# Attention and state-space block on one core: decays spread by DMA instead of by products with selecting rows

## The reference, cut to what matters

```python
dt = softplus(zxbcdt[..., -NHEADS:] + dt_bias)          # per token and head
A = -jnp.exp(A_log)
def step(state, inp):
    dt_t, x_t, B_t, C_t = inp
    dA = jnp.exp(dt_t * A)                               # the decay of this token, per head
    state = state * dA[:, :, None, None] + (dt_t[:, :, None] * x_t)[..., None] * B_t[:, None, None, :]
    y_t = jnp.einsum('bhpn,bn->bhp', state, C_t)
```

## Time and profile before

| | |
|---|---|
| median of 3 runs | 303.43 us (301.35 to 304.26) |
| the profiled execution | 301.26 us, span of its instructions 299.2 us |
| TensorE busy | 270.4 us, 90% |
| VectorE busy | 247.0 us, 83% |
| ScalarE busy | 207.6 us, 69% |
| GpSimd busy | 105.1 us, 35% |
| moved by DMA | 7.32 MB |

### The profile page before, as it was taken

How to read it: one execution, slowest core, us unless ns; L and a number is a source line. 1 busy time by engine, 2 the same in 40 slices (tenths; PEclk the granted TensorE clock), 3 DMA queues, 4 the chain that set the end, 5 groups by cost and what they waited for, 6 DMA issues and landing times.

```text
span 299.2 us, 6186 instructions
## 1 busy us (share of the span) xinstructions
PE 270.4 (90%) x2006; PEld 226.1 (76%) x2006; DVE 247.0 (83%) x537; ACT 207.6 (69%) x406; POOL 105.1 (35%) x113
## 2 busy tenths in 40 slices
PE   3999998999979999999999999997999897967781
PEld 3878996897868878887888788986798884555681
DVE  6695658787999979786899788858999999999943
ACT  1346779869868876968977787768674579777252
POOL 7000115600180614334333237116010519554552
PEclk9999999999999999999999999999999999999996
DMA  6910000000000000000000000000000100000103
GB/s 175 412 59 3 0 3 0 2 0 0 2 2 3 0 2 0 2 0 3 1 2 0 2 0 1 3 2 0 2 0 0 41 33 2 0 2 1 70 2 141
DMA packets 3787, 7.32 MB, mean 24 GB/s; under 512 B 652, under 2 KB 1581, under 8 KB 3757
## 3 DMA queue, kind: packets, MB, share of 16 engines
q1 hardware_dynamic: 3212, 6.72, 6.0%
q10 hardware_dynamic: 544, 0.21, 0.3%
HBM read 4.83 MB, written 2.10 MB: 23 GB/s over the span
## 4 chain that ended last, share of the span: by engine, by line
PE 66%; DVE 17%; issue 8%; ACT 5%; POOL 3%; DVEq 0%; ACTq 0%; POOLq 0%
PE mamba L1075 20%; PE scores L1075 17%; PE attn_out L1075 15%; PE turn L1148 7%; PE turn L1075 3%; DVE L L990 2%; DVE neg_max L900 2%; DVE th L1027 1%; DVE sp_sum L795 1%; POOL pre L524 1%; PE mamba L1166 1%; PE mamba L1207 1%; DVE L L1002 1%; DVE scanned L1010 1%; DVE res L911 1%
## 5 line engine op out<-in xcount | busy, mean ns | idle before, releaser
L1075 PE MATMUL attn_out<-values,pT 128*128 128x129 f32 x512 | 65.8, 276 | 2.5 <-DVE res L911 2.4
L1075 PEld LDWEIGHTS attn_out<-values,pT 128*128 128x128 f32 x512 | 62.2, 191 | 7.3 <-issue 4.9
L598 ACT ACTIVATE probs<-scores,neg_max 128x512 f32<-128x512 f32 x64 | 42.9, 686 | 24.6 <-DVE neg_max L900 22.2
L900 DVE TENSOR_REDUCE neg_max<-scores 128x1 f32<-128x1024 f32 x32 | 38.9, 1216 | 10.1 <-PE scores L1075 9.5
L990 DVE TENSOR_TENSOR_SCAN L<-mamba,ident 128x512 f32<-128x512 f32 x32 | 38.7, 1216 | 5.9 <-PE mamba L1075 5.7
L604 ACT ACTIVATE pT<-turn 128x512 f32<-128x512 f32 x64 | 37.6, 596 | 6.5 <-PE turn L1148 6.4
L1148 PE MATMUL turn<-ident,probs 128*128 128x128 f32 x256 | 37.9, 274 | 0.4 <-issue 0.2
L1148 PEld LDWEIGHTS turn<-ident,probs 128*128 128x128 f32 x256 | 30.2, 142 | 5.4 <-issue 3.2
L1075 PE MATMUL scores<-h_hi,q_hi 128*128 128x512 f32 x64 | 28.8, 451 | 2.7 <-ACT probs L598 1.2
L524 POOL TENSOR_TENSOR pre<-pre,th 128x512 f32<-128x512 f32 x16 | 20.7, 1292 | 27.6 <-ACT pre L630 22.2
L1075 PE MATMUL scores<-h_hi,q_lo 128*128 128x512 f32 x64 | 25.3, 395 | 0.0
(11 more groups left out here) (204 smaller groups left out, 613.9 us busy)
## 6 DMA issues: line engine op xcount, KB each, us to landing
res<-in_x_tok SPq DMA_DIRECT2D x4, 512.0 KB, 8.2
out<-res SPq DMA_DIRECT2D x8, 256.0 KB, 2.0
x_all<-in_x SPq DMA_DIRECT2D x3, 512.0 KB, 8.6
x_all<-in_x SPq DMA_DIRECT2D x2, 256.0 KB, 3.1
winT<-in_in_wT SPq DMA_DIRECT2D x1, 194.0 KB, 7.0
wqkv<-in_qkv_w ACTq DMA_DIRECT2D x1, 192.0 KB, 4.1
wpT<-in_proj_wT SPq DMA_DIRECT2D x1, 64.0 KB, 3.6
ob_row<-in_proj_b SPq DMA_DIRECT2D x1, 64.0 KB, 6.2
```

The source lines that it names most:

```text
L598: act.activation(probs[:, i % 2, half_of(h)], scores[:, half_of(h)], ACT.Exp, bias=neg_max[:, i:i + 1]).then_inc(exp_done.sem, 1)
L900: V.tensor_reduce(neg_max[:, n:n + 1], scores[:, :], AX.X, ALU.max, negate=True).then_inc(max_ready.sem, 1)
L1075: return T.matmul(o, w, v, start=start, stop=stop)
```

## The change

The decays are transposed on TensorE directly from dA, without the split in two parts. ScalarE copies the 32 rows (16 decays, 16 decays since the chunk's start, each of 128 tokens) to SBUF ("rows"), SyncE stores them to a scratch in DRAM ("wr", 16 KB), and per chunk one DMA reads four of the rows, 2 KB, and writes them to all 128 partitions of L, 256 KB ("bc"). The scan "l" reads L and writes L in place. For decay_in four DMAs per half batch ("dd", 64 KB each) write each head's rows to its 32 partitions. The zero at the start of each head now comes from the exponential: a bias of -1000 on the first partition, that is on the first token of a chunk. The steps dA_rows, dA_T, L, Dec and decay, the selecting rows and the mask are gone. ORDER is written anew throughout, with wr, bc, dd and the stores of the result ("store") as steps of SyncE, and other banks.

```diff
+                if kind == "wr":
+                    wait(sp, rows_ready, b, n + 1)
+                    sp.dma_start(rows_d[b, n], decay_rows[:, n, :]).then_inc(rows_out[n].sem, 16)
+                elif kind == "bc":
+                    wait(sp, rows_out[n // QUAD], b, 16)
+                    wait(sp, filled["Y"], b - 1, n // QUAD + 1)
+                    c = n % QUAD
+                    sp.dma_start(L[:, HEADS * n:HEADS * (n + 1), :].rearrange("p h i -> p (h i)"),
+                                 rows_d[b, n // QUAD, HEADS * c:HEADS * (c + 1), :].rearrange("(a h) i -> a (h i)", a=1)
+                                 .broadcast_to([P, HALF])).then_inc(spread[n].sem, 16)
+                elif kind == "dd":
+                    wait(sp, rows_out[n], b, 16)
+                    wait(sp, yo_ready, b - 1, n + 1)
+                    for h in range(HEADS):
+                        sp.dma_start(decay_in[h * HEADDIM:(h + 1) * HEADDIM, half_of(n)].rearrange("d (c i) -> d c i", c=QUAD),
+                                     rows_d[b, n, R:2 * R, :].rearrange("(a c h) i -> h a c i", a=1, h=HEADS)[h]
+                                     .broadcast_to([HEADDIM, QUAD, P])).then_inc(decay_in_ready[n].sem, 16)
...
-                    act.activation(dA[:, n, 0:R], la[:, n, :], ACT.Exp, scale=1.0 / A_SCALE).then_inc(dA_ready.sem, 1)
+                    act.activation(dA[:, n, 0:R], la[:, n, :], ACT.Exp, bias=first[:, :], scale=1.0 / A_SCALE
+                                   ).then_inc(dA_ready.sem, 1)
...
-                elif kind == "decay":
-                    wait(act, yo_ready, b - 1, n + 1)
-                    bank = take(act, b, "Dec", n)
-                    act.activation(decay_in[:, half], bank[:, :], ACT.Copy).then_inc(decay_ready.sem, 1)
+                elif kind == "rows":
+                    wait(act, rows_out[n], b - 1, 16)
+                    bank = take(act, b, "DAT", n)
+                    act.activation(decay_rows[:, n, :], bank[0:2 * R, 0:P], ACT.Copy).then_inc(rows_ready.sem, 1)
...
-                elif kind == "dA_rows":
...
-                elif kind == "dA_T":
...
                 elif kind == "l":
-                    wait(dve, filled["Y"], b - 1, n // QUAD + 1)
-                    bank = take(dve, b, "L", n)
-                    V.tensor_tensor_scan(L[:, HEADS * n:HEADS * (n + 1), :].rearrange("p a b -> p (a b)"), bank[:, :],
-                                         ident4[:, :, :].rearrange("p a b -> p (a b)"), 0.0, ALU.mult, ALU.add
+                    wait(dve, spread[n], b, 16)
+                    chunk = L[:, HEADS * n:HEADS * (n + 1), :].rearrange("p a b -> p (a b)")
+                    V.tensor_tensor_scan(chunk, chunk, ident4[:, :, :].rearrange("p a b -> p (a b)"), 0.0, ALU.mult, ALU.add
                                          ).then_inc(l_ready.sem, 1)
...
                 elif kind == "DAT":
-                    wait(pe, dA_rows_step, b, 2 * n + 2)
+                    wait(pe, dA_ready, b, n + 1)
+                    wait(pe, dec_ready, b, n + 1)
                     bank, done = fill(pe, b, "DAT", n)
-                    T.transpose(bank[:, 0:P], dA_rows[:, n, :], ident[:, :]).then_inc(done, 1)
+                    T.transpose(bank[:, 0:P], dA[:, n, :], ident[:, :]).then_inc(done, 1)
...
-                elif kind == "Dec":
...
-                elif kind == "L":
```

More of the change, by code:

```diff
@@ L184, in build @@
         neg_half = sb("neg_half", [P, TILES])
[L185 to L188, removed]
+        first = sb("first", [P, 1])
         x_all = sb("x_all", [P, BATCH * TOKENS])
@@ L439, in _, with step @@
                 sp.dma_start(res[:, b, :, :], x_tok[b]).then_inc(res_in[b].sem, 16)
-            for b in range(BATCH):
-                for n in range(2):
+            def step(kind, n, b):
+                if kind == "wr":
[15 more added lines that the diff above has]
+                                     .broadcast_to([HEADDIM, QUAD, P])).then_inc(decay_in_ready[n].sem, 16)
+                elif kind == "store":
                     four = slice(QUAD * n, QUAD * (n + 1))
@@ L447, in _ @@
                     sp.dma_start(out[b][:, four, :], res[:, b, four, :]).then_inc(out_sent[n].sem, 16)
+            for kind, n, b, _ in STEPS:
+                step(kind, n, b)
             for n in range(2):
@@ L760, in _ @@
             V.tensor_scalar(center[:, :], ident[:, :], 1.0 / P, None, ALU.subtract)
-            rows = ident[:, 0:4 * R].rearrange("r (s k c h) -> r k s c h", s=2, k=2, c=QUAD)
-            for k in range(2):
-                V.tensor_reduce(row_head[:, k, :], rows[:, k].rearrange("r s c h -> r h s c"), AX.XY, ALU.add)
-                last = V.tensor_reduce(row_chunk[:, k, :], rows[:, k].rearrange("r s c h -> r c s h"), AX.XY, ALU.add)
-            step_done(last)
-            V.tensor_copy(pick_chunk[:, :], row_chunk[:, 0, :])
-            V.tensor_copy(head_sel[:, :, :], row_head[:, 1, :].unsqueeze(2).broadcast_to([P, HEADS, HEADDIM]))
-            V.tensor_copy(head_mask[:, :, 0], row_chunk[:, 1, :])
-            step_done(V.tensor_tensor(head_mask[:, :, 1:P], row_head[:, 0, :].unsqueeze(2).broadcast_to([P, HEADS, P - 1]),
-                                      row_chunk[:, 1, :].unsqueeze(2).broadcast_to([P, HEADS, P - 1]), ALU.add))
-            dve.wait_ge(consts_done.sem, 9 + TERMS)
-            def rows_split(rows, value, signal, b, n):
-                k = value.shape[1]
-                V.tensor_copy(rows[:, 0:k].bitcast(F32R), value).then_inc(signal.sem, 1)
-                wait(dve, signal, b, 2 * n + 1)
-                V.tensor_tensor(rows[:, k:2 * k], value, rows[:, 0:k], ALU.subtract).then_inc(signal.sem, 1)
+            step_done(V.tensor_scalar(first[:, :], ident[:, 0:1], FIRST_BIAS, None, ALU.mult))
+            dve.wait_ge(consts_done.sem, 9 + TERMS)
             def softplus(b, n, k):
@@ L947, in step @@
                         wait(dve, sp_step, b, SP_STEPS * n + k)
+                    if k == SP_DT - 1:
+                        wait(dve, xdt_ready, b - 1, n + 1)
                     if k == SP_STEPS - 1:
```

187 lines of the change are left out of this document (86 added, 101 removed).

## The result

The changed kernel takes **307.05 us** in the median of 4 runs (305.94 to 307.35), the kernel before 302.39 beside it (301.32 to 304.26): a ratio of 1.0141, 95% interval [1.0074, 1.0207]. It is slower by 1.4%. I had predicted 296 us and given "slower" 0.37. (Ratios here leave disturbed runs out, so that they can differ a little from the quotient of two medians.)

A forecast was written before the change was run, and what follows sets the result against it. TensorE was taken as the bound from 10 to 220 us, VectorE after 245. 301.3 - 9.6 - 0.5 - 2.1 - 0.7 + 4.5 + 2.0 = 294.9, raised to 296 for half the return to the median; range 285 to 340.

The forecast's parts named there:

- TensorE, removed: L and Dec products gone: -9.6 us before 220 us (three quarters of 12.8), -0.5 between 220 and 245.
- The way through DRAM: Longer path from decays to scan by store and spread, nearly covered by other work: +2 us, bounds 0 and +8.
- the queue that I had set at nothing: SP's queue: its extra stores, spreads and small transfers delay nothing that is needed sooner: 0.
- The shared reading: Scans with two SBUF inputs stall beside GpSimd, mostly from 248 to 271 us: +4.5 us, bounds 0 and +7.
- VectorE's removed copies: After 245 us, where VectorE is the bound, two masked copies and four small steps go: -2.1 us.
- The start: Without the selecting rows and mask, the statistics of x begin earlier: -0.7 us, bounds 0 and -1.3.
- The hot row: Rival: spreads are slow because 128 partitions read the same DRAM row; +43, 339 us; chance 0.28.
- its worst form: Spreads cost by bytes, 12 us each, making the queue itself the bound: over 450 us; chance 0.07.
- rival (2): More scans beside GpSimd, whose waits lengthen the convolution's chain: +7 on the forecast, 303 us, no change; chance 0.15.
- wrong altogether would be a new bound that I haven't priced: Closing sentence on what would refute the forecast; its example was the SP queue held by a wait; no size.

The follow-up runs named there:

- e5: Kernel before, old order, with the 32 L and 8 Dec products run over 16 columns instead of 512: 306.52 us, ratio 1.0074.
- e3: Kernel before, old order, without L and Dec products, masked copies or the way through DRAM; scan reads constant ident4: 309.63 us, ratio 1.0203.
- e12: Changed kernel without the way through DRAM (scan reads ident4 twice), with useless products added in TensorE's waits: 297.77 us, ratio 0.9820.
- e2: Kernel before, products and order kept, only the scan reads SBUF constant ident4 twice instead of PSUM and ident4: 308.57 us, ratio 1.0179.

## Why the prediction was wrong, step by step

**"TensorE, removed" (-9.6 and -0.5) failed, and decided the sign.** Three errors sit in it. The size: 494 ns is the length of a bar that overlaps the next; the step is 0.32 us, so that 26 products before 220 us were 8.3 us and not 12.8. The share that comes back: I took three quarters, and the pace of the rounds held nearly all of it. In e5, at full clock, 0.7 us had come back by the 28th row maximum; in e3, with no product time but 3.4 us at half clock on the way, it starts at 195.0 us, where before has 195.1; and in e12, new order, no way, waits filled, the last one starts at 224.7 against 226.3. And the clock, which no term had: I took TensorE's time as something that can only be given back, while half clock followed some of the waits that were left, 3.4 us of it in e5 and 6.8 us in the changed kernel's first profile. Alone, the shortening cost 0.7% (e5).

**The way through DRAM (+2, bounds 0 and 8)** measured 4.7 to 5.6 us: right in mechanism, inside its bounds, mis-sized. The spread took 3.7 to 3.9 us where my nearest rows gave 2.7 to 3.5, and the queue that I had set at nothing delayed it: the first spread is issued 0.9 us after its rows have landed (a store lands after 1.4 us, and transfers for decay_in stand between), and the results' stores stretched it to 5.6 us.

**The shared reading (+4.5)** is there, and its sum came near by luck. Five scans stall in the changed kernel, by 4.4 us, the longest at 2.32 us (forecast: up to 2.4), but two of them stand at 197 and 200 us and not at the end. In the old order, for which I had counted, two stall and not nine, and the whole edit cost 5.0 us (e2), clock and GpSimd's own waits included. What I missed is who else reads so: over all VectorE instructions with two SBUF inputs (the excess of each over the shortest of its form) the stalls grew from some 14 to 25 us. About half of the growth is the scans' own; most of the rest is the softplus's small steps, which the new order has moved beside GpSimd, and those are what TensorE waits for at 182 us. The prediction's "one SBUF input never collides" is too wide: la, with one, takes 1.18 us beside an addition, against 0.17. What the shared reading costs the end of the changed kernel I haven't isolated: no run puts the scan's input back into PSUM in the new order.

**VectorE's removed copies (-2.1)** can't be told from the order's own changes. VectorE without its stalls fell by some 13 us, where I had said about 10. **The start (-0.7)** failed: the statistics of x begin at 4.79 us and not at 4.88, behind a wait of 1.79 us, so 0.1 us came of it.

```profile
4.79 1.29 DVE L823 BATCH_NORM_STATS2 gn_raw<-x_all 128x6 f32<-128x512 f32 x2 [1.79 <-POOL sp_coef L504]
```

My reading of the row before was wrong: x's first load has landed at 3.8 us, but VectorE also waits for constants of GpSimd's, the last of which (sp_coef) is written at 4.70.

**The rivals.** The hot row (0.28, and 0.07 for its worst form) didn't happen: 128 partitions read one line of 2 KB, and 256 KB land in 3.9 us, with 0.6 us between landings where four are issued in a row (70.9 to 72.8 us). I had hung the upper end of the range on it. What did happen was none of my cases; its time, 307, lies next to rival (2), 303, for another reason. The sentence "wrong altogether would be a new bound that I haven't priced" named SP's queue; it was TensorE's clock.

With waits filled and without the way the kernel takes 297.8 us (e12). My sum without its +2 for the way gives 294, so even there 4 us are missing: that it lies near the 296 predicted for the whole change is luck.

## What to carry to other kernels

Before taking work from the busiest engine, look at whether anything but that engine sets the pace of the stretch, and read the granted clock over its waits. Here TensorE's time hardly came back, half clock followed some of its waits, and useless products in waits of 1.4 to 4 us made the changed kernel faster. Price a matmul by the step to the next one's start, not by its bar. And where a new order is planned with a change, the order has its own hazards: here it laid small VectorE steps beside GpSimd's additions and loads of decays beside stores of results, neither of which the change itself asks for.

## What the runs showed that I had not expected

- The same kernel, with the same wait of 2.77 us, ran on at 2.4 GHz in one execution and at 1.2 in the other; the two spans differ by 3.9 us. Against the 299.2 us of before, the one profile shows a cost of 6.1 us and the other one of 2.1; neither alone is the change's.
- Reading collisions stretch both sides: the scans to 2.32 us from 1.2, 16-column steps to 1.23 from 0.17, and a GpSimd addition at 197.8 us to 2.2 from 1.27.
- A way through DRAM from ScalarE's copy (269.62) to the scan (276.08) takes 6.5 us: 0.3 to the store's issue, 2.3 to the spread's, 3.8 to the scan.
